# Context loads on ScalarE's queue, and two chunks instead of four turned ahead of the first shared product

## The chip, the cores and the metric

The kernel runs on one core of one Trainium2 chip. The metric is the device time in microseconds (us) of one execution. The engines are named as in the profile: PE is TensorE, DVE is VectorE, ACT is ScalarE, POOL is GpSimd, SP is SyncE, which here only issues DMAs. PEld is the weight load of a matmul.

## The reference, cut to what matters

Two transformer-like layers over x of 16 x 256 x 256. The change lies in the second one.

```python
def _L1_xattn_ref(queries, keys, values, Wq, bq, Wk, bk, Wv, bv, Wo, bo):
    ...                                      # q, k, v projections
    q_fft = jnp.fft.rfft(q, axis=-1)
    k_fft = jnp.fft.rfft(k, axis=-1)
    corr = jnp.fft.irfft(q_fft * jnp.conj(k_fft), n=Lq, axis=-1)
    mean_value = corr.mean(axis=(1, 2))
    _, index = jax.lax.top_k(mean_value.mean(axis=0), TOP_K)
    ...                                      # values shifted by the best lags, weighted
    return out @ Wo + bo

def _moe_forward(x, Wfc_s, bfc_s, Wproj_s, bproj_s, Wr, Wfc, bfc, Wproj, bproj):
    shared = new_gelu(xf @ Wfc_s + bfc_s) @ Wproj_s + bproj_s
    logits = xf @ Wr
    ...                                      # softmax, top 2 of 8 experts, gate
    for e in range(N_EXPERTS):
        h = new_gelu(xf @ Wfc[e] + bfc[e]) @ Wproj[e] + bproj[e]
        routed = routed + h * gate[:, e:e + 1]
    return (shared + routed).reshape(Bb, Tt, C)

x = x + _L0_xattn_ref(ctx_1024, ctx_1024, _layernorm(x), mask, ...)
x = x + _L0_ffn_ref(_layernorm(x), ...)
x = x + _L1_xattn_ref(_layernorm(x), ctx_1024, ctx_1024, ...)
x = x + _L1_ffn_ref(_layernorm(x), ...)      # this is _moe_forward
```

## The kernel before

Four stages follow one another, with a barrier of all engines between them: `attention`, `quant_mlp`, `autocorrelation` and `moe`. Each engine has an instruction stream written out by hand, and the streams are tied by semaphores; a DMA is issued in the stream of its engine and waits there behind whatever that stream waits for.

**autocorrelation.** A loop over the 16 batches b (`walk`) turns the context rows into z and its frequencies zf. In one tick PE does `transposes(b + 1)` (line 1520, from the tile `c_rows`, two buffers), the product of batch b with wz (line 1532), and the frequency product of batch b - 1 (line 1541). ACT copies the turned rows out of PSUM (`columns`, line 1450) and then z (line 1446). DVE adds a bias to zf (line 1618). SP loads `ctx_in[s]`, the two buffers of `c_rows`, 256 KB for each batch (line 1392), once the transposes of the batch two earlier have freed the buffer.

In the same stage POOL cuts the expert weights into a high and a low fp16 half: 18 halves of 1 MB in four pieces each (lines 151, 153, 155), of which seven fall into this stage. SP issues for them `load_half` (line 132, 1 MB) and `store_half` (line 138, 1 MB). The load waits for POOL to have finished with the buffer that it overwrites, and the store for POOL to have finished the half. In the program of SP these pairs stand between the context loads, after batches 5, 7, 9, 11 and 14. After its cutting POOL adds a bias to X (line 1435), behind which the mixing of the stage's end waits (line 1704).

**moe.** The 4096 tokens are 16 chunks of 256. `turn(c)` transposes a chunk's normalised rows on PE into the half bank TURN (line 2090); `take(c)` on ACT copies it to fp32 (line 2025, for the router) and to fp16 (line 2026); DVE computes the low half from the bank (line 2212); `logits(c)` multiplies by the router's weights wr (line 2098). TURN is one buffer: the next `turn` waits until ACT and DVE have read it. Four chunks are turned first; then PE waits for the shared expert's weights w1 and w2, and in `one(n)`, the first product of the shared expert (line 2124, four groups of 12 matmuls), one further chunk is turned and its logits taken in each group. `second` is the second product (line 2137, 48 matmuls). The order on PE is one(0), one(1), second(0), one(2), second(1), one(3), and so on.

AHEAD says how many chunks are turned before the first, second, ... shared product. With all 16 logits there, DVE picks the experts (`picks`), during one(3); PE computes prefix sums (line 2159), and DVE the slot tables and the positions of the rows. POOL then scatters the rows to their slots (line 1979, 64 indirect DMAs, one after the other). SP stores the shared result of each chunk (`store_shared`, line 1937), loads expert weights (`first_weights`, lines 1917 and 1918, `second_weights`, lines 1924 and 1925) and the slots' rows (`slot_rows`, line 1933).

Then 39 slots are computed, one after the other: `rows_T` transposes a slot's rows on PE (line 2109), `first` and `second` are the two products, with the slot's expert. The tick of slot s does `rows_T` of slot s + 1, `first` of slot s, and `second` of slot s - 1. Slot 2 and every sixth after it have one tile of 128 rows, the others two. DVE weights the output (lines 2365, 2370), and POOL adds the rows to the output in HBM (line 1993), one indirect DMA for each tile; a slot's adds start when those of the slot before have landed. The first add also waits for all 16 shared stores.

Of the kernel before, what the change touches and what calls it, by code (L numbers as in the profile page):

```python
# [1280 lines left out]
def autocorrelation(nc, d, g, X, ident, banks, halves_dram):  # L1281
# [15 lines left out]
    with ExitStack() as ctx:  # L1297
# [89 lines left out]
        @block.sync  # L1387
        def _(sp):
            def load(b, s):

                wait(sp, c_tr, b - 1)
                sp.dma_start(ctx_in[s][:], rows[:, b, :, :]).then_inc(c_ctx[s], 16)

            n, halves = CUT_BESIDE_ATTENTION + CUT_BESIDE_MLP, 2 * (d["L1_ffn_Wfc"].shape[0] + 1)
            load_half(sp, d, g.cut, n + 1)
            store_half(sp, g.cut, halves_dram, n - 1)
            for b in range(NB):
                load(b, b % 2)
                if b in (5, 7, 9, 11, 14):
                    load_half(sp, d, g.cut, n + 2)  # L1400
                    store_half(sp, g.cut, halves_dram, n)
                    n += 1
            assert n == halves - 2
            for n in range(halves - 2, halves):
                store_half(sp, g.cut, halves_dram, n)
            for s in range(2):
                sp.wait_ge(g.cut["stored"][s], 16 * (halves // 2))

            sp.wait_ge(c_lw, 2)
            sp.dma_start(lag_dram, lag_w[:].rearrange("b a s -> b (a s)")).then_inc(c_ls, 16)  # L1410
            sp.wait_ge(c_ls, 16)
            for q in range(4):
                for k in range(NQ):
                    n = NB // 4
                    src = bass.AP(tensor=lag_dram.tensor, offset=q * n * 2 * S + S - P - k * P, ap=[[1, P], [2 * S, n], [1, S]])
                    sp.dma_start(mixT[:, q * n:(q + 1) * n, k, :], src).then_inc(c_mx[q], 16)
            for q in range(4):
                sp.wait_ge(c_mx[q], 32)
# [19 lines left out]
        def _(act):  # L1438
# [9 lines left out]
            def columns(b, s):  # L1448
                act.wait_ge(c_tr, b + 1)
                act.activation(turned(b), banks[0][:, s * 512:(s + 1) * 512].rearrange("p (k t) -> p k t", k=KC), ACT.Copy).then_inc(c_cT, 1)  # L1450
# [272 lines left out]
def moe(nc, d, g, X, ident, banks, halves_dram, out):  # L1723
# [12 lines left out]
    AHEAD = (4, 8, 12, 16)  # L1736
# [5 lines left out]
    with ExitStack() as ctx:  # L1742
# [99 lines left out]
        e_sa = sem("rows_added")  # L1842

# [43 lines left out]
        TURN = banks[3][:, 512:1024]  # L1887
# [6 lines left out]
        def _(sp):  # L1894
            sp.dma_start(wr[:], d["L1_ffn_Wr"].rearrange("(k p) e -> p k e", p=P)).then_inc(e_c, 16)
# [52 lines left out]
            for c in range(CHUNKS - 4, CHUNKS):  # L1948
                store_shared(c)
            first_weights(0, 1)  # L1950
            second_weights(0, 1)

            slot_rows(0, 2)
# [9 lines left out]
        def _(pool):  # L1963
# [4 lines left out]
            pool.wait_ge(e_c, 16 * 6)  # L1968
# [39 lines left out]
        def _(act):  # L2008
# [11 lines left out]
            def take(c):  # L2020
# [3 lines left out]
                src = TURN.rearrange("p (k t) -> p k t", k=KC)  # L2024
# [57 lines left out]
        def _(pe):  # L2082
            def turn(c):
                pe.wait_ge(e_xn, c + 1)
                if c >= 1:
                    pe.wait_ge(e_xh, c)
                    pe.wait_ge(e_xl, c)
                for k in range(KC):
                    for t in range(ST):
                        ins = pe.transpose(TURN[:, (k * ST + t) * P:(k * ST + t + 1) * P], xn[:, ST * c + t, k * P:(k + 1) * P], ident[:])  # L2090
# [53 lines left out]
            pe.wait_ge(e_c, 16 * 6)  # L2144
            for c in range(AHEAD[0]):
                turn(c)
                logits(c)
# [9 lines left out]
            pe.wait_ge(e_m, 1)  # L2157
            pe.wait_ge(e_set, 3)
# [25 lines left out]
        def _(v):  # L2184
# [24 lines left out]
            def low_half(c):  # L2209
                cols = slice(c * SLOT, (c + 1) * SLOT)  # L2210
                v.wait_ge(e_xh, c + 1)
                v.tensor_tensor(xnT[:, 1, :, cols], TURN.rearrange("p (k t) -> p k t", k=KC), xnT[:, 0, :, cols], ALU.subtract).then_inc(e_xl, 1)
# [116 lines left out]
            v.wait_ge(e_c, 16 * 6)  # L2329
# [173 lines left out]
```

## Time and profile before

| | us |
|---|---|
| median of 3 runs | 1262.49 (1261.14 to 1263.27) |
| profiled execution, its own time | 1261.24 |
| its span, first to last instruction | 1259.5 |
| autocorrelation begins | 460.4 |
| moe begins | 641.0 |
| first slot's product begins | 853.7 |
| PE busy | 1132.3 (90% of the span) |
| DVE, ACT, POOL busy | 836.5, 589.7, 573.2 |

The span is what the trace covers; the profiled execution's own time is 1.74 us longer. Positions in the trace are us from the start of the span.

### The profile page before, as it was taken

What the parts mean: (1) busy time and instruction counts of PE and PEld (TensorE: products, weight loads), DVE (VectorE), ACT (ScalarE), POOL (GpSimd) and SP (SyncE); (2) the same over time, 40 slices, a digit from 0 to 9 for tenths busy, and PEclk for the clock granted to TensorE, in tenths of its full rate; (3) what the DMA queues carried; (4) which work ended last, traced back from release to release, by engine and by line L of the source; (5) the groups of instructions that cost most, each with busy time, mean ns of one, the idle gap of its engine ahead of it and who ended that gap; (6) DMA issues with size and microseconds to landing.
All of it is one profiled execution on the core that took longest, in us unless ns stands there. A gap on an engine that the chain in (4) does not pass through costs nothing. (4 is left out here: it accounts for less than half of the span.)

```text
span 1259.5 us, 27660 instructions
## 1 busy us (share of the span) xinstructions
PE 1132.3 (90%) x9970; PEld 860.6 (68%) x9970; DVE 836.5 (66%) x2627; ACT 589.7 (47%) x1065; POOL 573.2 (46%) x644
## 2 busy tenths in 40 slices
PE   1699999998677979799979999998999999999995
PEld 0244455444423658677869888887999999998985
DVE  6899999898697752237645686545656666656653
ACT  1488888787553732235137433323333343333431
POOL 4788787786550039976000017741232323332323
PEclk9999999999798999899978999999999999999998
DMA  9778787886420026620459033326989889898883
GB/s 268 139 169 170 168 177 161 163 151 201 136 67 1 1 84 201 201 118 0 135 164 223 1 124 136 129 100 204 283 258 283 265 271 274 267 272 265 275 248 98
DMA packets 180761, 215.69 MB, mean 171 GB/s; under 512 B 91937, under 2 KB 163489, under 8 KB 168113
## 3 DMA queue, kind: packets, MB, share of 16 engines
q1 hardware_dynamic: 167360, 197.42, 54.2%
q0 software_dynamic: 13296, 16.92, 6.8%
q8 instruction: 60, 0.98, 0.3%
q14 instruction: 45, 0.36, 0.1%
HBM read 143.86 MB, written 50.38 MB: 154 GB/s over the span
## 5 line engine op out<-in xcount | busy, mean ns | idle before, releaser
L2137 PE MATMUL banks<-moe_w,moe_hT 128*128 128x256 f16 x2472 | 278.5, 273 | 0.0
L2137 PEld LDWEIGHTS banks<-moe_w,moe_hT 128*128 128x128 f16 x2472 | 241.6, 98 | 27.9
L2049 ACT ACTIVATE moe_hf<-banks,moe_b 128x256 f32<-128x256 f32 (+1 forms) x440 | 178.8, 458 | 169.6 <-PE banks L2124 168.6
L1993 POOL DMA_INDIRECT out_x<-moe_y,slot_owner x71 | 113.1, 1594 | 267.6 <-DMA out_x<-moe_y,slot_owner 200.9
L758 DVE CUSTOM_DVE_ANT_0 masked<-banks,mask_bias 128x256 f32<-128x256 f32 x512 | 185.9, 420 | 24.5 <-PE banks L580 20.6
L2124 PE MATMUL banks<-moe_rT,moe_w 128*128 128x256 f16 (+1 forms) x1872 | 194.0, 264 | 0.0
L2124 PEld LDWEIGHTS banks<-moe_rT,moe_w 128*128 128x128 f16 x1872 | 170.3, 98 | 17.7
L490 ACT ACTIVATE probsT<-banks 128x1024 f32<-128x1024 f32 x128 | 130.7, 1021 | 48.4 <-PE banks L611 48.3
L2242 DVE TENSOR_TENSOR moe_hT<-moe_hf,moe_hT 128x512 f16<-128x512 f32 (+1 forms) x220 | 145.2, 660 | 7.6
L580 PE MATMUL banks<-kT,qT 48*128 48x256 f16 x512 | 92.4, 286 | 42.3 <-DMA qT<-q_split 22.5
L1979 POOL DMA_INDIRECT slots_x<-moe_xn,pos x64 | 64.8, 1013 | 124.1 <-DVE pos L2320 104.9
L2240 DVE CAST moe_hT<-moe_hf 128x512 f16<-128x512 f32 (+1 forms) x220 | 91.2, 414 | 43.4 <-ACT moe_hf L2049 41.4
L151 POOL TENSOR_SCALAR half_rows<-half_rows 128x512 f32<-128x512 f32 x72 | 108.0, 1500 | 7.6 <-issue 6.4
L2033 ACT ACTIVATE moe_rT<-banks 128x512 f16<-128x512 f32 (+1 forms) x39 | 21.8, 559 | 176.7 <-PE banks L2109 176.7
L580 PEld LDWEIGHTS banks<-kT,qT 48*128 48x128 f16 x512 | 34.6, 96 | 99.6 <-issue 50.0
L2365 DVE SCALAR_TENSOR_TENSOR moe_y<-banks,moe_b 128x512 f32<-128x512 f32 (+1 forms) x39 | 25.1, 644 | 112.3 <-PE banks L2137 100.2
L2124 PE MATMUL banks<-moe_xnT,moe_w 128*128 128x256 f16 x768 | 90.5, 277 | 0.0
L155 POOL TENSOR_TENSOR half_parts<-half_rows,half_parts 128x512 f16<-128x512 f32 x72 | 84.6, 1175 | 6.2
L593 PE MATMUL banks<-qmT,kT 64*128 64x256 f16 x512 | 85.1, 278 | 0.0
L2124 PEld LDWEIGHTS banks<-moe_xnT,moe_w 128*128 128x128 f16 x768 | 76.4, 99 | 9.7
L1097 PE MATMUL banks<-xqT,w1T 128*128 128x512 bf16 x256 | 68.5, 399 | 11.7 <-DVE hidden_max L1218 5.4
L626 PE MATMUL banks<-probsT,v_ones 128*32 128x256 f32 x1024 | 69.4, 389 | 0.3 <-ACT qmT L497 0.3
(349 smaller groups left out, 1771.4 us busy)
## 6 DMA issues: line engine op xcount, KB each, us to landing
moe_w<-moe_halves SPq DMA_DIRECT2D x80, 1024.0 KB, 5.2
moe_halves<-half_parts SPq DMA_DIRECT2D x18, 1024.0 KB, 6.4
slots_x<-empty_row SPq DMA_DIRECT2D x1, 9230.0 KB, 44.5
moe_rows<-slots_x SPq DMA_DIRECT2D x32, 260.0 KB, 6.0
half_rows<-in_L_ffn_Wfc SPq DMA_DIRECT2D x8, 1024.0 KB, 8.6
half_rows<-in_L_ffn_Wproj SPq DMA_DIRECT2D x8, 1024.0 KB, 8.7
moe_b<-in_L_ffn_bproj SPq DMA_DIRECT2D x39, 128.0 KB, 6.3
ctx_rows<-in_ctx SPq DMA_DIRECT2D x16, 256.0 KB, 2.9
```

The source lines that it names most:

```text
L151: pool.tensor_scalar(rows[:, cols], rows[:, cols], WSCALE, None, ALU.mult).then_inc(w["cut"], 1)
L155: pool.tensor_tensor(parts[:, 1, cols], rows[:, cols], parts[:, 0, cols], ALU.subtract).then_inc(w["cut"], 1)
L490: act.activation(probsT[n % EXPS][:].rearrange("p j k q -> p (j k q)"), psum_t[n % 2][:], ACT.Exp, scale=SCALE).then_inc(s_exp, 1)
L580: ins = pe.matmul(psum_s[:, at:at + S], qT[b % 2][rows, hp, t * P:(t + 1) * P], kT[b % 3][rows, hp, :], start=(t == 0), stop=(t == NQ - 1))
L593: pe.matmul(psum_t[n % 2][:, at:at + S], kT[b % 3][rows, hp, k * P:(k + 1) * P], qmT[b % 2][rows, hp, :], start=(k == 0), stop=False)
L758: ins = v.tensor_tensor_reduce(masked[2 * j + t][:], psum_s[:, at:at + S], mask_bias[b % 2][:, t, :], 1.0 / SHIFT, -3e38, ALU.add, ALU.max ...
L1993: pool.indirect_dma_start(out=out_rows, out_offset=bass.IndirectOffsetOnAxis(ap=owner[:, s, t:t + 1], axis=0), in_=y[s % 2][:, t, :], in_o ...
L2049: ins = act.activation(hf[p][:, j, 0:width], src, ACT.Gelu_apprx_tanh, bias=b1[buffer][:, j:j + 1], scale=1.0 / WSCALE)
L2124: ins = pe.matmul(banks[jp // 2][:, at:at + width], w1[buffer][:, w, k, j * P:(j + 1) * P], moving(x, k), start=(k == 0 and (w, x) == PART ...
L2137: ins = pe.matmul(OUT[p][:, t * D:(t + 1) * D], hT[p][:, x, j, t * P:(t + 1) * P], w2[buffer][:, w, j, :], start=(j == 0 and (w, x) == PAR ...
L2240: v.tensor_copy(hT[p][:, 0, at, 0:width], hf[p][:, at, 0:width]).then_inc(e_hh, 1)
L2242: v.tensor_tensor(hT[p][:, 1, at, 0:width], hf[p][:, at, 0:width], hT[p][:, 0, at, 0:width], ALU.subtract).then_inc(e_hl, 1)
```

## The change

It has six parts.

- The context loads: SP issues only the first two, at the head of the stage; the other 14 are issued by ACT in `columns`, after its wait for the transposes that free the buffer and ahead of its copy. SP issues the pairs of `load_half` and `store_half` with nothing between them.
- The router's weights wr have a semaphore of their own. PE waits for it after turn(0), and for the other five constants only ahead of the prefix sums.
- AHEAD is (2, 6, 10, 14, 16) in place of (4, 8, 12, 16), so ROUTED is 4: one(3) still turns two chunks, and the picks fall into one(4).
- The two chunks turned first use two half banks (`turn_bank`), so turn(1) doesn't wait for the copies of chunk 0.
- SP's order after the first two slots' rows is: stores 12 and 13, first_weights(0, 1), stores 14 and 15, slot_rows(0, 2), second_weights(0, 1). Before it was: stores 12 to 15, first_weights(0, 1), second_weights(0, 1), slot_rows(0, 2).
- The waits of POOL and DVE for the constants count five and not six.

```diff
-            def load(b, s):
-                wait(sp, c_tr, b - 1)
-                sp.dma_start(ctx_in[s][:], rows[:, b, :, :]).then_inc(c_ctx[s], 16)
+            for b in range(2):
+                sp.dma_start(ctx_in[b][:], rows[:, b, :, :]).then_inc(c_ctx[b], 16)
...
-            for b in range(NB):
-                load(b, b % 2)
-                if b in (5, 7, 9, 11, 14):
-                    load_half(sp, d, g.cut, n + 2)
-                    store_half(sp, g.cut, halves_dram, n)
-                    n += 1
+            for _ in range(5):
+                load_half(sp, d, g.cut, n + 2)
+                store_half(sp, g.cut, halves_dram, n)
+                n += 1
...
                 act.wait_ge(c_tr, b + 1)
+                if b + 2 < NB:
+                    act.dma_start(ctx_in[s][:], rows[:, b + 2, :, :]).then_inc(c_ctx[s], 16)
                 act.activation(turned(b), ...)
...
-    AHEAD = (4, 8, 12, 16)
+    AHEAD = (2, 6, 10, 14, 16)
...
-        TURN = banks[3][:, 512:1024]
+        def turn_bank(c):
+            return banks[2][:, 512:1024] if c < AHEAD[0] and c % 2 else banks[3][:, 512:1024]
...
-            sp.dma_start(wr[:], ...).then_inc(e_c, 16)
+            sp.dma_start(wr[:], ...).then_inc(e_wr, 16)
...
-            for c in range(CHUNKS - 4, CHUNKS):
+            for c in range(CHUNKS - 4, CHUNKS - 2):
                 store_shared(c)
             first_weights(0, 1)
+            for c in range(CHUNKS - 2, CHUNKS):
+                store_shared(c)
+            slot_rows(0, 2)
             second_weights(0, 1)
-            slot_rows(0, 2)
...
             def turn(c):
                 pe.wait_ge(e_xn, c + 1)
-                if c >= 1:
-                    pe.wait_ge(e_xh, c)
-                    pe.wait_ge(e_xl, c)
+                free = c if c >= AHEAD[0] else c - 1
+                if free >= 1:
+                    pe.wait_ge(e_xh, free)
+                    pe.wait_ge(e_xl, free)
...
-            pe.wait_ge(e_c, 16 * 6)
             for c in range(AHEAD[0]):
                 turn(c)
+                if c == 0:
+                    pe.wait_ge(e_wr, 16)
                 logits(c)
...
             pe.wait_ge(e_m, 1)
+            pe.wait_ge(e_c, 16 * 5)
             pe.wait_ge(e_set, 3)
```

## Rows read from the trace of the kernel before

**Rows 1.** Waits of PE, 460 to 565 us: us in total, times, longest
```profile
PE banks L1520 <- DMA c_rows<-in_ctx: 15.4, 5, 6.3
```

**Rows 2.** Windows: length, busy us PE, PEld, DVE, ACT, POOL, PE's clock, DMA share, GB/s
```profile
481.25:542.24 60.99, 49.50 (x241) 42.02 (x240) 16.24 (x36) 14.37 (x24) 57.17 (x54) 0.94 0.67 219
502.51:506.42 3.91, 3.91 (x21) 3.42 (x20) 1.35 (x3) 1.20 (x2) 3.76 (x4) 1.00 0.35 91
506.42:518.50 12.08, 5.81 (x22) 4.63 (x21) 1.35 (x3) 1.20 (x2) 11.55 (x12) 0.72 0.60 194
```

**Rows 3.** Timeline, head of the loop: start, length, engine, line, operation
```profile
467.86 0.40 DVE L1613 TENSOR_TENSOR bias_bc<-banks,bo_bc 128x256 f32<-128x256 f32 x1
470.17 1.87 PE L1520 MATMUL banks<-flip,c_rows 128*128 128x128 f32 x8 [3.96 <-DMA c_rows<-in_ctx]
...
477.34 1.90 PE L1541 MATMUL banks<-z,dft_flipped 128*128 128x257 f32 x8
```

**Rows 4.** Timeline of SP's queue around 504 us
```profile
504.25 1.62 SPq L1392 DMA_DIRECT2D c_rows<-in_ctx  x2
```

**Rows 5.** Timeline of ACT in one plain tick
```profile
483.62 0.60 ACT L1450 ACTIVATE vp<-banks 128x512 f32<-128x512 f32 x1 [1.57 <-PE banks L1520]
485.36 0.60 ACT L1446 ACTIVATE z<-banks 128x514 f32<-128x514 f32 x1 [1.14 <-PE banks L1532]
```

**Rows 6.** The tile c_rows, its 16 loads, from issue to landing
```profile
DMA to landing us min/median/max: 2.6/6.3/10.4
```

**Rows 7.** DMA issues, median us to landing: 1236 to 1260, then 1100 to 1236 us
```profile
out_x<-moe_y,slot_owner POOLq DMA_INDIRECT x5, 3.8
...
out_x<-moe_y,slot_owner POOLq DMA_INDIRECT x26, 6.8
```

**Rows 8.** Timeline: POOL's last cut piece, two bias adds, DVE's lag weights
```profile
556.05 1.16 POOL L155 TENSOR_TENSOR half_parts<-half_rows,half_parts 128x512 f16<-128x512 f32 x1
...
591.11 1.41 POOL L1435 TENSOR_TENSOR X<-X,bias_bc 128x256 f32 x2 [0.48 <-ACT x_rows L1469]
...
603.24 0.60 DVE L1671 TENSOR_SCALAR lag_w<-lag_e,first 16x256 f32<-16x256 f32 x2
```

**Rows 9.** Timeline, head of the moe stage
```profile
645.24 0.76 SPq L1904 DMA_DIRECT2D moe_b<-in_L_ffn_bproj_s  x1
...
645.52 1.11 PE L2090 MATMUL banks<-ident,moe_xn 128*128 128x128 f32 x4 [6.15 <-DMA tokens<-in_tokens]
...
659.57 1.09 PE L2090 MATMUL banks<-ident,moe_xn 128*128 128x128 f32 x4
```

**Rows 10.** DMA issues, 640 to 700 us: KB each, us to landing
```profile
moe_b<-in_L_ffn_bproj_s SPq DMA_DIRECT2D x1, 128.0 KB, 8.1
```

**Rows 11.** Windows: turning and half clock, one(2) with four chunks, second(1)
```profile
659.60:668.20 8.60, 8.60 (x43) 7.10 (x43) 2.50 (x4) 5.91 (x11) 0.00 (x0) 0.50 1.07 255
...
690.22:700.85 10.63, 10.60 (x99) 9.99 (x98) 7.33 (x12) 9.01 (x20) 0.00 (x0) 1.00 0.01 2
700.85:706.10 5.25, 5.25 (x51) 4.71 (x51) 1.12 (x2) 0.22 (x1) 0.00 (x0) 1.00 0.00 0
```

**Rows 12.** Timeline, from the shared products to the slots
```profile
838.93 0.35 POOL L1985 COPY slot_owner<-moe_rows 128x2 int32<-128x2 int32 x1 [4.20 <-DMA moe_rows<-slots_x]
...
850.84 0.60 PE L2109 MATMUL banks<-ident,moe_rows 128*128 128x128 f32 x4
...
853.67 5.40 PE L2124 MATMUL banks<-moe_rT,moe_w 128*128 128x256 f16 x48
...
856.32 1.01 SPq L1933 DMA_DIRECT2D moe_rows<-slots_x  x2
...
863.30 0.69 PE L2109 MATMUL banks<-ident,moe_rows 128*128 128x128 f32 x2 [4.22 <-DMA moe_rows<-slots_x]
...
870.21 5.40 PE L2137 MATMUL banks<-moe_w,moe_hT 128*128 128x256 f16 x48
```

**Rows 13.** Timeline of POOL: an add that waits for DVE's output
```profile
998.39 1.55 POOL L1993 DMA_INDIRECT out_x<-moe_y,slot_owner  x1 [6.75 <-DVE moe_y L2370]
```

More of the change, by code:

```diff
@@ L1842, in moe @@
         e_sa = sem("rows_added")
+        e_wr = sem("router_weights_in")
         block = ctx.enter_context(nc.Block())
@@ L1894, in _ @@
         def _(sp):
-            sp.dma_start(wr[:], d["L1_ffn_Wr"].rearrange("(k p) e -> p k e", p=P)).then_inc(e_c, 16)
+            sp.dma_start(wr[:], d["L1_ffn_Wr"].rearrange("(k p) e -> p k e", p=P)).then_inc(e_wr, 16)
             sp.dma_start(before[:], d["before"]).then_inc(e_c, 16)
@@ L1967, in _ @@
             pool.memset(ones[:], 1.0).then_inc(e_set, 1)
-            pool.wait_ge(e_c, 16 * 6)
+            pool.wait_ge(e_c, 16 * 5)
             pool.tensor_copy(xn[:, :, TOKEN].bitcast(I32), tokens[:]).then_inc(e_meta, 1)
@@ L2023, in take @@
                     act.wait_ge(e_l, c - 1)
-                src = TURN.rearrange("p (k t) -> p k t", k=KC)
+                src = turn_bank(c).rearrange("p (k t) -> p k t", k=KC)
                 act.activation(xT32[c % 2][:], src, ACT.Copy).then_inc(e_tc, 1)
@@ L2084, in turn @@
                 pe.wait_ge(e_xn, c + 1)
-                if c >= 1:
-                    pe.wait_ge(e_xh, c)
-                    pe.wait_ge(e_xl, c)
+                free = c if c >= AHEAD[0] else c - 1
+                if free >= 1:
+                    pe.wait_ge(e_xh, free)
+                    pe.wait_ge(e_xl, free)
                 for k in range(KC):
                     for t in range(ST):
-                        ins = pe.transpose(TURN[:, (k * ST + t) * P:(k * ST + t + 1) * P], xn[:, ST * c + t, k * P:(k + 1) * P], ident[:])
+                        ins = pe.transpose(turn_bank(c)[:, (k * ST + t) * P:(k * ST + t + 1) * P], xn[:, ST * c + t, k * P:(k + 1) * P], ident[:])
                 ins.then_inc(e_t, 1)
@@ L2211, in low_half @@
                 v.wait_ge(e_xh, c + 1)
-                v.tensor_tensor(xnT[:, 1, :, cols], TURN.rearrange("p (k t) -> p k t", k=KC), xnT[:, 0, :, cols], ALU.subtract).then_inc(e_xl, 1)
+                v.tensor_tensor(xnT[:, 1, :, cols], turn_bank(c).rearrange("p (k t) -> p k t", k=KC), xnT[:, 0, :, cols], ALU.subtract).then_inc(e_xl, 1)
             moments()
@@ L2328, in _ @@
                     shared_output(n - 1, (n - 1) % 2)
-            v.wait_ge(e_c, 16 * 6)
+            v.wait_ge(e_c, 16 * 5)
             picks()
```

## The prediction

> **What bounds the kernel now.** PE is busy for 90% of the span, so the first question is where it stands idle, and what ends that. I read the waits of PE over the autocorrelation loop, then windows over the loop's ticks, then SP's queue for what stood ahead of the late transfer. The waits show one cause: PE waits for context rows, five times, 15.4 us in all [rows 1]. The windows show the price with the clock in it. A plain tick is 3.91 us, all of it PE work. Twelve ticks from 481.25 to 542.24 take 60.99 us where 12 x 3.91 are 46.9, so 14.1 us are lost in the middle of the loop; the worst tick took 12.08 us, and behind its long wait PE ran at 1.2 GHz for a while (mean 0.72) [rows 2]. The queue shows why: SP could issue two context loads only at 504.25 [rows 4], because it had been standing in the pair of half-weight transfers that waits for POOL, and they then moved behind those 2 MB. Landing times of context loads run from 2.6 us, nothing ahead, to 10.4 us [rows 6].
>
> In the moe stage I read the timeline at its head and then at the seam between shared products and slots. PE stands idle 6.15 us until the last of six small constants has landed, turns four chunks in 659.57 - 645.52 = 14.05 us, that is 3.5 us each, at 1.2 GHz, and only then begins one(0) [rows 9]. At the seam PE waits 4.22 us for slot 2's rows, which SP issued only at 856.32 [rows 12]. Between and after these places PE is full. In the slot phase adds and PE run at nearly the same pace; at 998.39 POOL still waits for DVE's output and through it for PE [rows 13], so what PE gains before the slots reaches the end.
>
> **Context loads on ACT.** Head of the loop: SP's first load no longer stands behind 2 MB. It lands some 3 us after 460.4, and the transposes start when DVE's last copy ends, 467.86 + 0.40 = 468.3, in place of 470.17 [rows 3]. The idle gap shrinks to about 2 us. The three short waits of the loop, (15.4 - 4.0 - 6.3) / 3 = 1.7 us each [rows 1, 3], kept 2.4 GHz: nearly all that the loop's mean of 0.94 lacks is in the 12.08 us tick [rows 2]. So from there at 2.4 GHz: transposes 0.65, ACT's issue about 0.5, its copy 0.6, the product 1.75, z's copy 0.75, the second product 1.8: the first frequency product at 474.5, where it was at 477.34. That is 2.8 us.
>
> Middle of the loop: 14.1 us go if each load lands in time. A load starts when a batch is turned and is wanted two ticks later, 7.8 - 0.6 = 7.2 us [rows 2]. Without traffic it lands in 2.6 us [rows 6]. Beside SP's 2 MB on a queue of its own the trace has no hardware-issued load, so I bound it. POOL's adds of 128 KB, on another queue than SP's, land in 3.8 us alone and in 6.8 us beside the expert loads [rows 7], 3.0 us more. The load is 256 KB: 2.6 + 3.0 = 5.6 at the low end, and no stall; 2.6 + 6.0 = 8.6 at the high end, a stall of 1.4 at each of five pairs, 7 us. I take the low end, as rows 7 show a transfer beside another queue's traffic and not behind it, and charge 0.5 us.
>
> The Trainium skill speaks for and against ("DMA: Bandwidth & Descriptors"). "Issuing engines are not separate DMA queues" says that DMAs started by several engines share the same 16 DMA engines and that this saves only the issue time; taken alone it makes the loads as late as before. "Queues, rings and completion order" gives SP and ACT a ring each on every DMA engine, served in turn by packets; by that they land early. Rows 7 agree with the second, for POOL's ring.
>
> ACT pays 14 issues. It is idle 1.57 + 1.14 = 2.71 us in a tick [rows 5]; SP's issues take up to 0.76 us [rows 9], so they are hidden, and would cost at most 14 x 0.76 = 10.6 us if ACT had no cover. Queued behind an issue are the copy of the turned rows, wanted by PE only in the next tick, and z's copy, which has 1.14 us to spare.
>
> What is late next? POOL's cutting doesn't get shorter: it ends at 557.2. Its 32 bias adds are then 16 x 1.41 = 22.6 us back to back, so it is done at 579.8; the first reader behind them comes after the lag weights, 603.84 - 16.4 = 587.4 [rows 8]. 7.6 us are left, so POOL costs nothing. Sum for this part: 2.8 + 14.1 - 0.5 = **16.4 us**.
>
> **Head of moe.** PE no longer waits for the constants; two chunks at the old 3.5 us would be done by 652.6 even if begun only at 645.52, and they can begin 3 us earlier. But one(0) also waits for w1, w2 and their biases. The last of these lands 8.1 us after its issue at 645.24, at 653.3 [rows 9, 10]. This is DMA time from the stage's head, which the change doesn't touch. So one(0) begins at 653.3 and not at 659.57: 6.2 us. The second turn bank and wr's own semaphore lie under the same wait and are worth nothing beyond it; without that cover they would be worth the 6.15 us of rows 9. Two more chunks must now be turned among the products: a shared product with four chunks takes 10.63 us and one of 48 matmuls alone 5.25, so a chunk costs 1.35 us and two cost 2.7 [rows 11]. Before, one(0) ran 8.6 us at 1.2 GHz [rows 11]; PE now comes to it out of an idle stretch and I take the same 8.6. If the clock came back at once, 4.3 us would be gained besides; if twice as late, 4.3 lost. Net **3.5 us**.
>
> **Routing one chunk later.** The picks stand one first and one second product, 10.5 us, later in PE's order, and so do the 64 scatters. Slot 0's rows had arrived at 838.93, and PE took them up at 850.84: a margin of 11.9 us [rows 12], of which 1.4 are left. SP's stores, waiting behind the scatters, come 7 us later in time but still before their use. Cost nothing, with 1.4 us to spare.
>
> **SP's order at the seam.** Slot 2's rows are issued right behind the last store, and w1 of slot 1 ahead of it. first(0) starts at 853.67 and ends at 858.9; in the old order, rows_T(2) then waits until 863.30 and first(1) runs partly at 1.2 GHz, so second(0) starts at 870.21 [rows 12]. Without the wait it is 858.9 + 0.25 + 5.25 = 864.4: **5.8 us**. The rows are issued about 853 (old frame); even 4.2 us to landing, in the range of rows 6, is before 858.9. second_weights(0, 1) falls 1 us behind the rows, and is wanted only at the second product after, over 15 us on.
>
> Sum: 16.4 + 3.5 + 5.8 = 25.7 us. Against the profiled execution's own time, 1261.24, that is 1235.5; against the median of the runs, 1.25 us above it, 1236.8. I say **1236 us**.
>
> **Rivals.**
> - *The loads still queue behind the halves.* For it: every late load so far did, and the rule on issuing engines above. Against: rows 7. Landing 8.7 to 10.4 us after 7.2 us of cover is 1.5 to 3.2 us at five pairs, about 10 more than charged: 1246 us.
> - *The slots' rows come late.* The margin of 1.4 us is thin; should scatters or DVE's tables run 4 us later, PE waits 2.6 us: 1239 us.
> - *The clock comes back early in one(0).* Elsewhere PE regained 2.4 GHz sooner: the 12.08 us tick has mean 0.72 [rows 2]. Half of the 4.3 us: 1234 us.
> - *No change:* the loop's gain is waited away at POOL's bias adds and the moe gain at the scatters. It needs the 7.6 us to be gone and 16 us more. Nothing in the profile points there: 1262 us.
> - *Slower: issuing on ACT stalls ACT.* Place: in `columns`, between the wait and the copy. An indirect issue on POOL takes 1.55 us [rows 13], still under the 2.71 of idle time. Beyond the cover each issue costs 14 times its excess; 25.7 / 14 = 1.8 us of excess undo all gains, so above about 4.5 us per issue the kernel is slower. At 6 us it would be 14 x 3.3 - 25.7 = 20.5 us slower, 1282 us.
>
> **How the numbers follow.** Forecast 0.62 (own range 1233 to 1240), loads behind the halves 0.17, late rows 0.07, early clock 0.07, no change 0.03, slower 0.04. The range reaches down to the early clock with 3 us for the bounds, 1230, and up to the first rival, 1247. A difference under 0.2% (2.5 us) is about what this measurement can't tell from none. Every case but the last two is faster by over 0.2%: 0.93; same 0.03; slower 0.04.
>
> **What the profile of the changed kernel would show.** PE's wait for c_rows near 0; ticks of 3.91 throughout, and the moe stage beginning near 624.6; context landings under 7.2 us. One(0) starting 12.3 us after the stage's head, with PE idle some 5 us before it. PE's wait for slot 2's rows gone, and a wait for slot 0's rows of nothing. It goes wrong if context loads land after 7.2 us, if POOL's bias adds become what the mixing waits for, or if PE waits at the seam for slot 0.

## The result, and the profile after

The changed kernel takes 1244.61 us in the median of 4 runs (1241.97 to 1246.87), the kernel before, run beside it, 1261.82 us in the median of 4 (1259.19 to 1263.27): a ratio of 0.9865, with a 95% interval of 0.9839 to 0.9892. It is 17.2 us faster, where 1236 us, 25 us less, was forecast. 1244.61 lies inside the range of 1230 to 1247, and outside the likeliest case's own 1233 to 1240; it is nearest to the first rival's 1246.

The profiled execution has 1241.97 us of its own (span 1240.0), 19.3 us below that of before (1261.24). Its times can be laid beside those of before, stretch by stretch (the stage with the loop starts at PE's first instruction in it, moe at SP's first issue):

| stretch | before, us | after, us | gained | forecast |
|---|---|---|---|---|
| start of the stage with the loop to the first frequency product | 16.9 | 15.7 | 1.2 | 2.8 |
| first to sixteenth frequency product | 71.3 | 61.6 | 9.7 | 13.6 |
| from there to the head of moe | 92.4 | 93.2 | -0.8 | 0 |
| head of moe to the first add | 236.9 | 227.0 | 9.8 | 9.3 |
| first add to the end | 381.6 | 381.5 | 0.1 | 0 |

Waits of PE from 455 to 560 us, in the columns of [rows 1]. Context rows now hold it up for 3.9 us, where it was 15.4.

```profile
PE banks L1517 <- DMA c_rows<-in_ctx: 3.9, 4, 1.9
PE banks L1517 <- DVE bias_bc L1610: 2.1, 1, 2.1
```

The tile c_rows again, and the DMA queues (packets, MB, share of 16 engines). The 14 loads issued by ACT have a queue of their own, q10, which the kernel before doesn't have; SP's transfers are on q1.

```profile
DMA to landing us min/median/max: 2.7/4.7/9.2
```
```profile
q1 hardware_dynamic: 163552, 193.75, 54.3%
q0 software_dynamic: 13296, 16.92, 7.1%
q10 hardware_dynamic: 3808, 3.67, 0.9%
```

Windows, in the columns of [rows 2]: the same twelve ticks, the worst tick among them, and two pieces of the loop's head. Twelve ticks take 51.27 us, 4.3 more than 12 x 3.91, and the clock stays at 2.4 GHz throughout, where [rows 2] has 60.99 us and a tick at a mean of 0.72. The last two lines are at 1.2 GHz in part and in full.

```profile
480.63:531.90 51.27, 47.61 (x241) 40.80 (x240) 16.23 (x36) 14.36 (x24) 48.88 (x47) 1.00 0.61 203
508.76:514.79 6.03, 4.14 (x22) 3.34 (x21) 1.35 (x3) 1.20 (x2) 5.80 (x6) 1.00 0.61 233
470.00:472.00 2.00, 1.31 (x4) 1.11 (x5) 0.00 (x0) 1.19 (x2) 1.85 (x3) 0.77 0.84 293
472.00:474.00 2.00, 2.00 (x5) 1.12 (x4) 0.00 (x0) 0.00 (x0) 1.93 (x3) 0.50 0.63 220
```

Timeline of that worst tick. SP issues a pair (1 MB in, 1 MB out) at 502.55 and 502.96; ACT issues a context load at 503.31, 0.35 us behind the second. PE can turn these rows at 512.55, 9.2 us later. The cover of two buffers is 7.2 us; PE waits 1.89 us.

```profile
502.55 0.37 SPq L132 DMA_DIRECT2D half_rows<-in_L_ffn_Wproj  x1
502.96 0.58 SPq L138 DMA_DIRECT2D moe_halves<-half_parts  x1
503.31 0.37 ACTq L1446 DMA_DIRECT2D c_rows<-in_ctx  x1
...
512.55 0.66 PE L1517 MATMUL banks<-flip,c_rows 128*128 128x128 f32 x4 [1.89 <-DMA c_rows<-in_ctx]
```

There are five such pairs, 13.5 us apart, at POOL's pace of cutting: SP issues their first halves at 475.56, 489.05, 502.55, 516.05 and 529.55. In the steady part of the loop exactly one load behind each of the middle three is late: issued at 490.83, 503.31 and 517.16, usable after 7.9, 9.2 and 8.6 us. The ticks lengthen by 0.75, 2.12 and 1.47 us; the other loads land in time. The first pair's next load comes 3.5 us behind it, at 479.09, and the fifth has none behind it: ACT issues its last load at 521.07. The late loads land with the pair ahead of them: the second halves of the three pairs take 8.7, 9.2 and 8.9 us from issue to landing and are there some 0.4 to 0.6 us before PE can turn the rows.

Head of the loop, timeline. The transposes begin at 468.85, as DVE's copy ends, 7.8 us after the stage's start (before: 9.7). But PE had stood still for 2.10 us, works 1.09, stands 0.74 for ACT's copy, and the product behind it takes 3.44 us where 1.97 is usual.

```profile
468.85 1.09 PE L1517 MATMUL banks<-flip,c_rows 128*128 128x128 f32 x8 [2.10 <-DVE bias_bc L1610]
...
470.69 3.44 PE L1529 MATMUL banks<-wz,vp 128*128 128x257 f32 x8 [0.74 <-ACT vp L1447]
474.36 0.70 PE L1517 MATMUL banks<-flip,c_rows 128*128 128x128 f32 x4 [0.24 <-DMA c_rows<-in_ctx]
...
476.72 1.46 PE L1538 MATMUL banks<-z,dft_flipped 128*128 128x257 f32 x6
```

Head of moe, timeline, and a window of one(0)'s first part: the transposes ahead of one(0) start 12.1 us behind SP's first issue, out of 3.83 us idle, and run at 1.2 GHz for 8.3 us. (In the kernel before SP's first issue of the stage is at 641.0, so by [rows 9] one(0) starts 18.6 us behind it; [rows 11] have 8.6 us at 1.2 GHz.)

```profile
631.42 0.38 SPq L1895 DMA_DIRECT2D wr<-in_L_ffn_Wr  x1
...
632.59 0.66 PE L2093 MATMUL banks<-ident,moe_xn 128*128 128x128 f32 x4 [2.78 <-ACT moe_xn L2019]
...
643.56 1.09 PE L2093 MATMUL banks<-ident,moe_xn 128*128 128x128 f32 x4 [3.83 <-issue]
```
```profile
643.56:651.90 8.34, 8.34 (x40) 6.86 (x41) 2.51 (x4) 4.95 (x10) 0.00 (x0) 0.50 1.09 281
```

The seam, timeline. Slot 0's rows are there for POOL at 835.91 and PE takes them up at 837.28: a margin of 1.4 us. Slot 2's rows are issued at 839.91, POOL can read them at 844.82, and PE turns them at 845.36 without a wait, 0.5 us later. From first(0), 840.12, to second(0), 850.81, are 10.7 us, where [rows 12] have 870.21 - 853.67 = 16.5.

```profile
835.91 0.19 POOL L1987 COPY slot_owner<-moe_rows 128x2 int32<-128x2 int32 x1 [4.25 <-DMA moe_rows<-slots_x]
...
837.28 0.60 PE L2112 MATMUL banks<-ident,moe_rows 128*128 128x128 f32 x4
...
839.91 0.34 SPq L1933 DMA_DIRECT2D moe_rows<-slots_x  x1
840.12 5.40 PE L2127 MATMUL banks<-moe_rT,moe_w 128*128 128x256 f16 x48
...
844.82 0.19 POOL L1987 COPY slot_owner<-moe_rows 128x1 int32<-128x1 int32 x1 [7.80 <-DMA moe_rows<-slots_x]
...
845.36 0.38 PE L2112 MATMUL banks<-ident,moe_rows 128*128 128x128 f32 x2
...
850.81 5.40 PE L2140 MATMUL banks<-moe_w,moe_hT 128*128 128x256 f16 x48
```

### The profile page after: what moved, and what is told of

Its sections match the earlier page's. It is cut to its first block and busy times, and to the rows that moved or that the text cites. A ratio compares the mean times of both kernels' runs of the same rounds, so it can differ in the third digit from the quotient of the medians.

```text
span 1240.0 us, 27660 instructions
## 1 busy us (share of the span) xinstructions
PE 1125.0 (91%) x9970; PEld 853.4 (69%) x9970; DVE 837.4 (68%) x2627; ACT 588.5 (47%) x1065; POOL 571.2 (46%) x644
```

## The experiments

Twelve kernels in three batches, each beside the kernel before. In batches A and B the kernel before took 1339.07 (1334.93 to 1341.26) and 1339.70 us (1332.62 to 1344.13), in batch C 1263.18 (1260.99 to 1264.96), though B and C ran on the same chip. Times are therefore compared inside a batch only; across batches, stretches that are alike in both. The changed kernel itself ran in batch C but not in A or B. So where an expectation for A or B names a difference from the changed kernel, only a stretch of the profile can answer it, not the total.

**Batch A: the change in parts.** The first kernel has the loads on ACT and nothing else of the change, the second all of the moe stage and no loads on ACT.

loads_only, beside the changed kernel:
```diff
-    AHEAD = (2, 6, 10, 14, 16)
+    AHEAD = (4, 8, 12, 16)
...
-            for c in range(CHUNKS - 4, CHUNKS - 2):
+            for c in range(CHUNKS - 4, CHUNKS):
                 store_shared(c)
             first_weights(0, 1)
-            for c in range(CHUNKS - 2, CHUNKS):
-                store_shared(c)
-            slot_rows(0, 2)
             second_weights(0, 1)
+            slot_rows(0, 2)
...
+            pe.wait_ge(e_c, 16 * 6)
             for c in range(AHEAD[0]):
                 turn(c)
-                if c == 0:
-                    pe.wait_ge(e_wr, 16)
                 logits(c)
```
The second turn bank is gone with them.


> The kernel before with the context loads moved to ACT's queue and nothing else of the change. Theory (the two halves of the change are independent and add): the stage autocorrelation takes about 170.4 us, as in the changed kernel, where it took 180.6 before, so about 10 us less than the kernel before, a ratio of 0.992. The moe stage takes its old 618.5 us. Rival (the time of the moe stage depends on when POOL's and SP's earlier work ended): the moe stage's length changes by over 1 us.

moe_only, beside the changed kernel:
```diff
-            for b in range(2):
-                sp.dma_start(ctx_in[b][:], rows[:, b, :, :]).then_inc(c_ctx[b], 16)
+            def load(b, s):
+                wait(sp, c_tr, b - 1)
+                sp.dma_start(ctx_in[s][:], rows[:, b, :, :]).then_inc(c_ctx[s], 16)
...
-                if b + 2 < NB:
-                    act.dma_start(ctx_in[s][:], rows[:, b + 2, :, :]).then_inc(c_ctx[s], 16)
```
SP's calls of load stand again between its pairs.


> The changed kernel with the context loads back on SP between the pairs. Theory (independent halves): the stage autocorrelation takes its old 180.6 us and the moe stage 608.6 us where it was 618.5, so about 10 us less than the kernel before, a ratio of 0.992. Rival (parts overlap in what they save): less than 8 us.

Loads alone: 1326.92 us (1320.01 to 1333.16), ratio 0.9894 (0.9858 to 0.9931). Moe alone: 1326.97 us (1323.62 to 1327.91), ratio 0.9904 (0.9878 to 0.9929). 12 us each. The stage with the loop takes 170.8 us with loads alone and 181.2 with moe alone, as against 170.4 and 180.5 in the profiles of after and before: its gain of 10 us is that of the loads, and is theirs alone. The moe stages, for which 618.5 and 608.6 us were expected, took 698.9 and 681.9; they can't be compared with those of after, for a reason told in the last section. So it is shown that the gain of the loads needs nothing of the moe half; what the moe half gains by itself is not.

third_buffer: a third buffer for context rows, so that a load is issued three ticks before its rows are wanted and not two. The third buffer counts its loads on a semaphore that the mixing uses later, and the mixing's counts are raised to match.
```diff
-        ctx_in = [sb(f"c_rows{s}", [P, NQ, D]) for s in range(2)]
+        ctx_in = [sb(f"c_rows{s}", [P, NQ, D]) for s in range(3)]
...
-            for b in range(2):
+            for b in range(3):
...
-                if b + 2 < NB:
-                    act.dma_start(ctx_in[s][:], rows[:, b + 2, :, :]).then_inc(c_ctx[s], 16)
+                if b + 3 < NB:
+                    act.dma_start(ctx_in[b % 3][:], rows[:, b + 3, :, :]).then_inc(c_ctx[b % 3], 16)
```


> The changed kernel with three buffers for the context rows in place of two, each load asked for one tick earlier. Theory (a load issued just behind a pair of half transfers lands after 9.2 us, and two ticks cover only 7.2): cover rises by 3.9 to 11.1 us, PE's waits for context rows inside the loop go to 0, and 4.3 us are saved against the changed kernel. Rival (the DMA engines lack the bandwidth in this stage, so an earlier issue only queues earlier): the waits stay, 0 to 1 us saved.

1316.19 us (1310.54 to 1317.32), ratio 0.9820 (0.9788 to 0.9853). The stage took 166.3 us, 4.1 less than after. The tile c_rows, then a window over all 15 intervals of the loop:

```profile
DMA to landing us min/median/max: 2.7/3.8/7.9
```
```profile
479.36:536.60 57.24, 56.25 (x286) 48.88 (x284) 19.77 (x44) 18.05 (x29) 54.63 (x52) 1.00 0.65 206
```

57.24 us where after has 61.55, and no wait of PE for c_rows inside the loop. So the 4.3 us left in the loop were landings beyond the cover of two buffers, and nothing that ACT, DVE or the products do. That the longest landing is 7.9 us here is not the reason: in all_three and all_and_loop, with the same three buffers, it is 9.0 and 8.9, and the loop takes 57.23 us all the same. ACT's 13 issues cost nothing here either.

old_seam: SP's order at the seam as before, all else changed.
```diff
-            for c in range(CHUNKS - 4, CHUNKS - 2):
+            for c in range(CHUNKS - 4, CHUNKS):
                 store_shared(c)
             first_weights(0, 1)
-            for c in range(CHUNKS - 2, CHUNKS):
-                store_shared(c)
-            slot_rows(0, 2)
             second_weights(0, 1)
+            slot_rows(0, 2)
```


> The changed kernel with SP's old order at the seam: stores 12 to 15, then w1 and w2 of slot 1, then slot 2's rows. Theory: PE waits 4.2 us for slot 2's rows again and runs part of the next product at 1.2 GHz; from first(0) to second(0) 16.5 us in place of 10.7, so 5.8 us slower than the changed kernel, and the end moves by as much, as PE sets the pace. Rival (the slot phase's end is set by POOL's chain of adds, which starts late anyway): the seam loses 5.8 us, the end less than 3.

1324.03 us (1322.96 to 1327.49), ratio 0.9899 (0.9873 to 0.9924). Timeline at its seam; first(0) began at 915.64:

```profile
918.29 0.84 SPq L1933 DMA_DIRECT2D moe_rows<-slots_x  x2
...
924.77 0.44 PE L2110 MATMUL banks<-ident,moe_rows 128*128 128x128 f32 x2 [3.73 <-DMA moe_rows<-slots_x]
925.05 7.07 PE L2125 MATMUL banks<-moe_rT,moe_w 128*128 128x256 f16 x48
...
931.95 5.40 PE L2138 MATMUL banks<-moe_w,moe_hT 128*128 128x256 f16 x48
```

The wait and the slow product of [rows 12] are back, and the way from first(0) to second(0) is 16.3 us, 5.6 more than with the new order. First add to the end is 381.6 us, as in the kernels with the new order, so what the seam lost reached the end; the total can't say it, as the changed kernel is not in this batch. Its loop lost only 1.3 us to late loads, where after lost 4.3. Part of that is where the loads fall: behind its pairs of 493.71, 507.24 and 520.75 the next loads come 2.4, 0.9 and 3.6 us later (1.8, 0.8 and 1.1 in after). The rest is not explained: for a load 0.9 us behind a pair PE waited 0.4 us here, for one 0.8 us behind it 1.9 in after.

**Batch B: the sizes that were chosen.**

three_ahead: three chunks turned before one(0), not two.
```diff
-    AHEAD = (2, 6, 10, 14, 16)
+    AHEAD = (3, 7, 11, 15, 16)
```


> The changed kernel with AHEAD (3, 7, 11, 15, 16). In the changed kernel PE ends its two chunks 8.3 us after the moe stage's head and then stands idle 3.8 us until the shared weights are in, at 12.1. Theory (the head is bound by the weights' transfer, not by turning): a third chunk fits into the idle time, one(0) still begins 12.1 us after the head, and the chunk no longer costs 1.35 us among the products: 1.35 us less up to the first slot. Rival (turning bounds the head): one(0) begins up to 3.5 us later and the kernel is 2 us slower.

1317.59 us (1315.84 to 1319.47), ratio 0.9836 (0.9796 to 0.9875). Its moe stage takes 681.7 us, as against 681.9 in moe_only and 682.6 in early_turn, which have two chunks. One(0)'s first transposes:

```profile
648.67 1.09 PE L2093 MATMUL banks<-ident,moe_xn 128*128 128x128 f32 x4 [2.08 <-issue]
```

The stage's head was at 634.51, so one(0) begins 14.2 us behind it, and PE still stood 2.08 us with three chunks turned. With two chunks it begins 12.1 us behind in after and 14.5 in changed_again. It is the shared expert's weights that set it: in changed_again the last of their biases is issued at 638.28 and takes 9.9 us to landing, and PE begins at 648.31. A third chunk fits under that wait. What it is worth stays open: this profile ran one(0) at 1.2 GHz for 9.2 us, those of moe_only and early_turn for 3.8 and 3.4, and the slow shared products of this batch vary by more than the 1.35 us that were expected.

early_turn: batch 0 is turned as soon as its rows and the first weight product are there.
```diff
-            pe.wait_ge(c_wr, 4)
+            pe.wait_ge(c_wr, 1)
...
+                    if b == 0:
+                        pe.wait_ge(c_wr, 4)
                     pe.wait_ge(c_cT, b + 1)
```


> The changed kernel, PE transposing the first two batches of context rows when DVE has made the first of its four copies, not the last. In the changed kernel the first frequency product begins 15.7 us after PE's first instruction of the stage, 1.2 us earlier than before where 2.8 were forecast, and PE ran at 1.2 GHz there. Theory (the clock fell because PE stood idle 2.1 us and then 0.7): the idle time shrinks, the copies are ready 1.2 us earlier, and the clock holds, which gives another 1.5 us: 13.0 us. Rival (the clock falls for the light work of this place whatever the gap): only the 1.2 us, 14.5 us.

1320.21 us (1314.02 to 1326.69), ratio 0.9873 (0.9826 to 0.9920), and the first frequency product 16.9 us behind the stage's start, no sooner than in the kernel before, where 13.0 was expected. Timeline of its head:

```profile
465.36 1.09 PE L1517 MATMUL banks<-flip,c_rows 128*128 128x128 f32 x8 [0.86 <-DVE wz L1608]
...
466.05 0.44 ACTq L1446 DMA_DIRECT2D c_rows<-in_ctx  x1
...
467.28 1.97 PE L1531 MATMUL banks<-wz,vp 128*128 128x257 f32 x8 [0.83 <-ACT vp L1447]
472.16 1.11 PE L1517 MATMUL banks<-flip,c_rows 128*128 128x128 f32 x4 [2.90 <-DMA c_rows<-in_ctx]
473.07 2.81 PE L1531 MATMUL banks<-wz,vp 128*128 128x257 f32 x8
```

The first step did what was meant: with 0.86 and 0.83 us idle before it, in place of 2.10 and 0.74, the product ran in 1.97 us and not 3.44. What came next was late in its turn: batch 2's rows, issued at 466.05 by ACT behind the pair that SP had issued at 459.68 and 460.18, with the DMA engines 98% busy from 466.00 to 468.90, were there 6.1 us later, and the clock fell after that wait of 2.90 us (mean 0.50 from 472 to 474).

five_routed: the picks yet one chunk later.
```diff
-    AHEAD = (2, 6, 10, 14, 16)
+    AHEAD = (2, 6, 10, 14, 15, 16)
```


> The changed kernel with AHEAD (2, 6, 10, 14, 15, 16): the same turning, but the picks one more chunk later, in one(5). In the changed kernel slot 0's rows are in 1.4 us before PE takes them. Theory (each chunk of delay takes 10.5 us from that margin): PE waits for slot 0's rows about 9.1 us at the seam, and the kernel is 9 us slower than the changed one. Rival (scatters overlap or slot rows have hidden slack): under 4 us slower.

1316.30 us (1313.98 to 1318.46), ratio 0.9832 (0.9791 to 0.9873). The scatters start 127.1 us behind the head of moe, where after has 116.2, and PE does not wait for slot 0's rows. The expected loss of 9 us didn't come in this batch: the shared products themselves ran so slowly (last section) that POOL could read slot 0's rows at 878.05 and PE took them up at 909.79, a margin of 31.7 us, the same as in moe_only (891.64 to 923.34). Whether the margin of 1.4 us gives way where the products run at full pace was not tried.

all_three: the edits of third_buffer, early_turn and three_ahead together.
```diff
-    AHEAD = (2, 6, 10, 14, 16)
+    AHEAD = (3, 7, 11, 15, 16)
...
-        ctx_in = [sb(f"c_rows{s}", [P, NQ, D]) for s in range(2)]
+        ctx_in = [sb(f"c_rows{s}", [P, NQ, D]) for s in range(3)]
...
-            pe.wait_ge(c_wr, 4)
+            pe.wait_ge(c_wr, 1)
```


> The changed kernel with the third buffer for context rows, three chunks turned ahead, and the early transposes. Theory (the parts lie one after another on PE's path and add): 4.3 + 1.35 + 1.2 to 2.7 = 6.9 to 8.3 us less than the changed kernel, which is 24 to 26 us less than the kernel before. Rival (a downstream bound, such as POOL's bias adds ahead of the mixing, takes over): under 5 us.

1312.51 us (1311.13 to 1315.65), ratio 0.9807 (0.9767 to 0.9847): 27 us less than the kernel before, where 24 to 26 were expected. The first frequency product comes 13.1 us behind the stage's start and the loop takes 57.23 us: with batch 2's rows loaded by SP ahead of the pair, early_turn gives what was expected of it.

**Batch C: a return to 1263 us, and one more question.** These four were made to ask why the shared products ran slowly in A and B. In this batch no kernel had that slow stretch, as in the first runs, so they answer something else.

changed_again: the changed kernel, nothing edited.

> The changed kernel itself, beside the kernel before, on whatever chip this is. Where the kernel before takes 1262 us, it should take 1244 again (the loop 170 +/- 3, moe 608.6). Where the kernel before takes 1339 us, the parts run alone say: loads alone gave 12 us, moe alone 12 us, five ways of both 16 to 26 us; so some 18 us less than before, 1321 us, autocorrelation near 170, moe near 684, and PE standing in many short waits for issue in the shared products while POOL issues its 64 scatters (from some 116 us behind the head of moe on, for some 83 us).

1244.14 us (1242.27 to 1245.83), ratio 0.9845 (0.9826 to 0.9864): the first result again. Its profiled execution, the slowest of its four, lost 5.9 us in the loop, 5.4 of them at one load (5.1 in its tick and 0.3 in the next). The window of that tick, and PE's wait in it:

```profile
508.44:517.45 9.01, 5.49 (x22) 4.26 (x21) 1.35 (x3) 1.20 (x2) 8.63 (x9) 0.85 0.59 188
```
```profile
513.85 0.66 PE L1517 MATMUL banks<-flip,c_rows 128*128 128x128 f32 x4 [3.52 <-DMA c_rows<-in_ctx]
```

The load came 10.8 us after its issue, as long as the pair's second half ahead of it took; after 3.52 us of waiting the clock fell (mean 0.85 in the tick), after 1.89 us at the same place in the profile of after it had not.

pe_loop: PE's code for the last shared products as a loop of two chunks.
```diff
-            for n in range(ROUTED + 1, CHUNKS):
+            LOOPED = 2 * ((ROUTED + 2) // 2)
+            for n in range(ROUTED + 1, LOOPED):
...
+            with pe.Fori(LOOPED // 2, CHUNKS // 2) as i:
+                for q in range(2):
+                    one(2 * i + q)
+                    second(2 * i + q - 1, 1 - q, SHARED)
```


> The changed kernel with PE's shared products from chunk 6 on in a loop of two chunks in place of straight code: the same products, fewer instructions to bring. Theory A (on these chips PE is starved of instructions that have to be fetched, while POOL issues indirect transfers): the 40 us of waits for issue at the first shared product and the 22 at the second vanish, first add comes near 236 us behind the head of moe, where it is at 300, and the kernel is some 60 us faster than the changed one: 1255 to 1265 where the kernel before takes 1339. Theory B (it is contention at the products themselves, or something else that meets PE whatever its code): no change, 1320 +/- 4. Where the starvation is absent (kernel before at 1262): 1244 to 1247, the loop's own branches being the only difference.

1242.47 us (1239.74 to 1245.31), ratio 0.9830 (0.9808 to 0.9851). No difference from changed_again that these runs can tell. Its profile has a moe stage 3.4 us longer (613.5 and 610.1), but not through the loop: PE waits 0.56 us for slot 2's rows, and the head loses 2.6 us more, as one(0) runs at 1.2 GHz for some 9.3 us, where it was some 3 in changed_again. Four transposes of one(0), pe_loop's 5.0 us behind its start, then changed_again's 4.0 us behind; 1.09 us is their time at 1.2 GHz, 0.64 at 2.4:

```profile
648.97 1.09 PE L2093 MATMUL banks<-ident,moe_xn 128*128 128x128 f32 x4
```
```profile
652.30 0.64 PE L2093 MATMUL banks<-ident,moe_xn 128*128 128x128 f32 x4
```

four_scatters: 60 of the 64 scatters are left out.
```diff
-            for i in range(2):
-                sp.wait_ge(e_sc[i], 8 * PICKS * NT)
+            sp.wait_ge(e_sc[0], 16 * FLIGHT)
...
-            for T in range(NT):
+            for T in range(2):
```


> The changed kernel with only the first 4 of POOL's 64 scatters, the other 60 left out: nearly all routed rows stay where they are, and the slots compute on what the memory holds. PE's work is the same. If the scatters are the cause, PE's waits for issue in the shared products vanish but for a few us, the shared products run at 10.5 us a pair, and the first add comes near 227 us behind the head of moe, where it is at 300: 1250 us. If they are not, the waits stay where they are in time and the kernel takes 1320.

1245.64 us (1243.99 to 1247.24), ratio 0.9858 (0.9839 to 0.9877). Here too nothing: where the slow stretch is absent, the 60 scatters cost PE nothing, neither by traffic nor at the seam. First add 228.4 us behind the head of moe, 228.5 in changed_again.

all_and_loop: all_three with pe_loop.

> Everything that helped so far together: three buffers for context rows, transposes of batch 0 ahead of the weights' last part, and PE's shared products in a loop. The first two gave 7 us more than the change alone (1312.5 beside 1320). By theory A the loop's gain adds to it, 1250 us where the kernel before takes 1339; by theory B nothing, 1312 us. Where the kernel before takes 1262: 1237.

1236.38 us (1235.34 to 1237.14), ratio 0.9786 (0.9769 to 0.9803): the fastest version, 7.8 us below changed_again, and none of its four runs overlaps with those. Head of its loop, and its seam:

```profile
470.36 1.98 PE L1533 MATMUL banks<-wz,vp 128*128 128x257 f32 x8 [0.83 <-ACT vp L1449]
472.17 0.60 PE L1519 MATMUL banks<-flip,c_rows 128*128 128x128 f32 x4
...
474.93 1.25 PE L1542 MATMUL banks<-z,dft_flipped 128*128 128x257 f32 x5
...
840.27 0.44 PE L2116 MATMUL banks<-ident,moe_rows 128*128 128x128 f32 x2 [1.20 <-DMA moe_rows<-slots_x]
```

In its profile the head is 2.8 us shorter than in that of changed_again (13.1 against 15.9), the loop 5.9 (57.23 against 63.16), the moe stage 0.5. The new wait of 1.20 us for slot 2's rows, and that of 0.56 in pe_loop, show how thin the cover at the seam is.

## Why the prediction was right, and where its sizes were off

The waits that the prediction named went, and for the reasons that it gave. Two terms of the loop were too large, and the term at the head of moe came out right with some luck. The time lies inside the stated range because the range was stretched to the first rival's 1247. Forecast 25.7, profile 19.3: 3.9 less in the middle of the loop, 1.6 less at its head, 0.8 lost behind it and 0.5 ahead of the stage, 0.6 more in moe, and 0.2 less in what lies around the span.

- **Middle of the loop (14.1 less 0.5).** The step that failed is the choice of the low bound, "5.6 at the low end, and no stall; 2.6 + 6.0 = 8.6 at the high end", and with it the charge of 0.5 us. The loss measured 4.3 us in after, 5.9 in changed_again, and between 1.3 and 6.0 in the other kernels with two buffers and these loads. The landing has two sizes, not one: 4.7 us in the median, and 7.9, 9.2 and 8.6 for a load issued right behind a pair. The row that it was nearest to, [rows 7], is a median over adds with no particular place in the traffic; here the place decides. The high end priced a stall of 1.4 us at each of five pairs. It came at three, at 1.45 on average, because the fifth pair has no load left behind it and the first has one only 3.5 us later; the sum overlooked that. The case "the loads still queue behind the halves" was the nearer one in the time it gave, 1246 us, and half right in its reason: a load right behind a pair landed with the pair although it had a queue of its own; all others were in time. third_buffer shows the size: more cover, and the 4.3 us are gone.
- The Trainium skill's "Issuing engines are not separate DMA queues" ("DMA: Bandwidth & Descriptors") says that DMAs of all issuing engines run on the same 16 DMA engines; the three late loads agree with it. Its "Queues, rings and completion order", which gives ACT a queue row of its own, agrees with the row of q10. Neither says alone what a tick will lose.
- **Head of the loop (2.8).** The transposes began nearly as forecast, 7.8 us behind the stage's start (7.9 forecast). The step that failed is "so from there at 2.4 GHz". It rested on three short waits of 1.7 us in the mean, which kept the clock; the gap here was 2.10 us and a second of 0.74 followed after 1.09 us of work. The product at 470.69 took 1.5 us longer and the rest slipped with it. (The forecast's own terms add up to 474.35 and not to its 474.5.) early_turn and all_and_loop show the gaps as the cause: with 0.86 and 0.83 us of idle time it takes 1.97 or 1.98 us. Which of the two gaps did it was not separated. The longest of the three waits had been 2.04 us, with full work before it, and kept 2.4 GHz:

```profile
526.35 0.66 PE L1520 MATMUL banks<-flip,c_rows 128*128 128x128 f32 x4 [2.04 <-DMA c_rows<-in_ctx]
```
- **ACT's issues (0).** Right. In a plain tick of after ACT still waits 1.99 us for the turned rows and 0.72 for z, an issue taking 0.38. The case of a slower kernel needed 4.5 us per issue.
- **POOL next (0).** Right. Its bias adds end at 582.9 and the lag weights are made at 593.6, 10.7 us of margin. They don't run back to back, but wait for ACT's x_rows, 4.0 us in all. It held even in all_and_loop, whose loop is 4.3 us shorter yet. The 0.8 us lost behind the loop are small: a wait of 0.44 us for ACT's copy is the largest.
- **Head of moe (3.5).** The two steps that make the sum came within 0.3 us in the first profile: one(0) starts 12.1 us behind the head (12.3 forecast) and the clock stays low for 8.3 (8.6). PE stood idle 3.83 us ahead of it, where some 5 were forecast, and up to the first slot's product the stage gained 4.0 us. That the clock took this long was luck: it is low for some 3 us in changed_again, for 9.3 in pe_loop, and between 2.8 and 9.3 over all profiles, and the wait ahead of it doesn't tell which (6.47 us in changed_again, 5.67 in pe_loop). The rival "the clock comes back early" is thus what nine of the thirteen kernels did. In changed_again it made up for weights that landed 2.4 us later.
- **Routing later (0, 1.4 us to spare).** Right: the margin measured 1.4 us, and 1.0 in changed_again (840.04 to 841.08). The runs don't show what a later pick costs, as five_routed met the slow shared products.
- **SP's order at the seam (5.8).** Right: 16.5 to 10.7 us, 5.8; undone in old_seam, 5.6 back. The cover is thinner than forecast: slot 2's rows came 4.9 us after their issue, where 4.2 had been allowed, and PE had 0.5 us to spare.

The median of the first runs of after lies 2.6 us above its profiled execution, that of before 0.6. No trace of the other three executions tells why; the loop's loss alone differs by 4.7 us between kernels whose loop is the same (1.3 to 6.0). So the forecast is 8.6 us off by medians, 6.4 by profiles.

## What to carry to other kernels

A transfer moved to an engine of its own escapes the other queue's waits, but not its bytes. Price it at the place it is issued: a load right behind a pair of 1 MB transfers took some three times as long as one alone (9.2 us, 2.7 the least), and a median hides that. When a wait goes but for a part, ask for the cover of the worst landing, here a third buffer, before asking for speed; with it, another edit that had given nothing (early_turn) gave its 2.8 us. An idle gap of PE can cost itself plus a slow stretch behind it; here a gap of 2.10 us and one of 0.74 with 1.09 us of work between them did, while single gaps of 1.89 and 2.04 us in full work did not.

## What the runs showed of the hardware that was not expected

**One chip, two times.** The same program took 1339.70 us in batch B and 1263.18 us in batch C on one chip. The kernel before has a profile from the first runs only, so where its 76 us lie is read from the others: nearly all in the shared products. Moe alone has its first add 300.3 us behind the head of the stage; the changed kernel 227.0 in after and 228.5 in changed_again; from the first add on they take 381.5 to 381.6 (loads_only takes 385.8, for a reason that stays open). Waits of PE from 735 to 960 us in loads_only, and a piece of its timeline, PE and POOL together:

```profile
PE banks L2121 <- issue: 40.2, 25, 3.8
PE banks L2134 <- issue: 22.6, 11, 2.4
```
```profile
807.15 0.96 POOL L1976 DMA_INDIRECT slots_x<-moe_xn,pos  x1 [0.30 <-issue]
808.41 0.96 POOL L1976 DMA_INDIRECT slots_x<-moe_xn,pos  x1 [0.30 <-issue]
808.72 0.37 PE L2134 MATMUL banks<-moe_w,moe_hT 128*128 128x256 f16 x1 [2.43 <-issue]
...
811.52 0.37 PE L2134 MATMUL banks<-moe_w,moe_hT 128*128 128x256 f16 x1 [2.43 <-issue]
...
814.32 0.37 PE L2134 MATMUL banks<-moe_w,moe_hT 128*128 128x256 f16 x1 [2.43 <-issue]
```

Single matmuls of 0.37 us stand 2.80 us apart, with nothing in the profile that PE waits for, and DVE and ACT get less to do in step. Windows of that stretch: PE busy for 33.83 of 96.80 us at a mean clock of 0.64. In the same 96.80 us of after it is busy throughout, at 1.00.

```profile
735.00:831.80 96.80, 33.83 (x221) 21.45 (x220) 18.94 (x41) 7.12 (x18) 62.43 (x64) 0.64 0.33 115
831.80:870.00 38.20, 38.18 (x330) 33.28 (x330) 19.82 (x35) 11.62 (x28) 0.00 (x0) 0.94 0.06 22
```

It goes with POOL's 64 scatters. In all eight kernels of A and B the first wait of this kind over 0.8 us comes 13 to 20 us after the first scatter is issued, and the last one 5 to 10 us after the last scatter (in five_routed too, whose scatters come 11 us later behind the head of moe). Together these waits are 46 us in five_routed and 54 to 60 in the other seven, and its moe stage is the shortest of the eight, 677.9 us. After and changed_again issue the same scatters at the same pace and have no such wait. That a shortage of instructions on PE is behind it was argued from the name of the wait and not shown: pe_loop and four_scatters were made to test that and ran in a batch without the slow stretch. The queue q8, of kind instruction, carries 60 packets in all eight as in after, so nothing more was brought in; whether it came late, no view tells. What brings the slow stretch about stays open too. A whole batch had it or had not, the kernel before and every variant alike, so comparisons inside a batch hold; lengths of the moe stage are not to be carried from one to another.
